# A transformer layer with 16 experts: each scatter of a sequence's sorted rows waits for the one before it

## The reference

```python
x = x + layernorm(attention(layernorm(x)))      # 16 heads, rotary positions, causal
x = x + layernorm(moe(layernorm(x)))

def moe(x):                                     # on n = 4096 tokens xf
    scores = sigmoid(xf @ gate_w.T)             # 16 experts in 4 groups
    # of the 4 groups the best 2 are kept, of their experts the best 4 (TOPK)
    topk_w = 2.5 * chosen / (chosen.sum() + 1e-20)
    hg, hu = xf @ Wg[e].T, xf @ Wu[e].T         # each expert: 256 -> 128
    y = sum over the 4 chosen e of topk_w * ((silu(hg) * hu) @ Wd[e].T)
    shared = (silu(xf @ Ws_g.T) * (xf @ Ws_u.T)) @ Ws_d.T
    return x + y + shared
```

## Time and profile before

| what | value |
|---|---|
| runs of the kernel, us | 983.48, 983.83, 987.33; median 983.83 |
| the profiled execution, span in us | 1048.8 |
| TensorE clock granted, mean | 0.888 of full speed |
| busy: PE / PEld / DVE / ACT / POOL, us | 852.6 / 615.2 / 652.3 / 456.3 / 426.7 |
| share of the span: PE / DVE / ACT / POOL | 81% / 62% / 44% / 41% |
| the scatters' DMA queue (q0): packets, MB | 13824, 38.55 |
| the other DMA queue (q1): packets, MB | 75248, 128.85 |

### The profile page before, as it was taken

How to read it: one execution, slowest core, us unless ns; L and a number is a source line. 1 busy time by engine, 2 the same in 40 slices (tenths; PEclk the granted TensorE clock), 3 DMA queues, 4 the chain that set the end, 5 groups by cost and what they waited for, 6 DMA issues and landing times.

```text
span 1048.8 us, 20609 instructions
## 1 busy us (share of the span) xinstructions
PE 852.6 (81%) x6580; PEld 615.2 (59%) x6580; DVE 652.3 (62%) x1914; ACT 456.3 (44%) x763; POOL 426.7 (41%) x408
## 2 busy tenths in 40 slices
PE   4569798987987987987987877978977799989955
PEld 3436374664664663664654545757865588867722
DVE  5577658687687687687586674533642233687916
ACT  2115454544544544544543555425433355544410
POOL 3222113135335335335213234374565555664621
PEclk9759898997897897997987998889999999998978
DMA  4685726236336336336395212453545566997783
GB/s 161 147 222 144 216 64 163 75 98 174 98 99 173 99 99 173 98 81 172 98 322 159 85 47 92 144 167 93 166 150 161 161 178 164 383 314 281 247 339 128
DMA packets 89175, 168.72 MB, mean 161 GB/s; under 512 B 14704, under 2 KB 56688, under 8 KB 88816
## 3 DMA queue, kind: packets, MB, share of 16 engines
q1 hardware_dynamic: 75248, 128.85, 42.1%
q0 software_dynamic: 13824, 38.55, 9.9%
HBM read 90.15 MB, written 76.68 MB: 159 GB/s over the span
## 4 chain that ended last, share of the span: by engine, by line
PE 40%; DVE 23%; issue 11%; SPq 8%; DMA 6%; another core or an unknown queue 5%; ACT 4%; POOL 3%; DVEq 0%; ACTq 0%; POOLq 0%
DVE nmax L829 8%; PE ring L1536 6%; PE ring L1314 5%; PE ring L1316 4%; PE ring L1315 4%; PE ring L1392 3%; PE ring L1557 3%; PE ring L1358 2%; SPq L628 2%; PE ring L1383 2%; SPq L629 2%; DMA xg<-sorted_rows 2%; PE ring L1436 2%; PE ring L1522 2%
## 5 line engine op out<-in xcount | busy, mean ns | idle before, releaser
L1244 ACT ACTIVATE prob<-ring 128x1024 f32<-128x1024 f32 (+1 forms) x192 | 167.5, 881 | 215.5 <-PE ring L1383 196.5
L829 DVE TENSOR_REDUCE nmax<-ring 128x2 f32<-128x1024 f32 (+3 forms) x256 | 201.8, 819 | 73.3 <-PE ring L1365 43.6
L736 POOL DMA_INDIRECT expert_rows<-ys,dest x160 | 159.2, 995 | 127.0 <-ACT ys L1198 74.8
L728 POOL DMA_INDIRECT sorted_rows<-xr,idx_all x128 | 130.5, 1019 | 104.8 <-DVE xr L991 71.5
L1536 PE MATMUL ring<-we,xh 128*128 x640 | 160.3, 396 | 0.0
L1536 PEld LDWEIGHTS ring<-we,xh 128*128 128x128 f32 x640 | 121.6, 200 | 14.6
L1054 DVE SCALAR_TENSOR_TENSOR sl<-sl,got,ring 128x128 f32<-128x128 f32 x160 | 48.3, 343 | 109.8 <-ACT sl L1296 62.5
L1358 PE MATMUL ring<-k_st,q_st 48*128 48x512 f32 (+3 forms) x512 | 88.9, 387 | 26.0 <-issue 9.7
L1392 PE MATMUL ring<-prob,v_sb 128*32 128x512 f32 (+3 forms) x1024 | 106.3, 518 | 3.2 <-ACT prob L1244 3.2
L1377 PE MATMUL ring<-maskt_b,halves_b 64*128 64x128 bf16 (+2 forms) x768 | 58.4, 233 | 50.7 <-DVE nmax L829 23.5
L1377 PEld LDWEIGHTS ring<-maskt_b,halves_b 64*128 64x128 bf16 x768 | 22.8, 97 | 125.4 <-issue 56.7
(11 more groups left out here) (203 smaller groups left out, 1650.8 us busy)
## 6 DMA issues: line engine op xcount, KB each, us to landing
xg<-sorted_rows SPq DMA_DIRECT2D x160, 134.0 KB
parts<-part SPq DMA_DIRECT2D x32, 512.0 KB
ykt<-expert_rows SPq DMA_DIRECT2D x14, 1024.0 KB
k_st<-parts SPq DMA_DIRECT2D x64, 128.0 KB
q_st<-parts SPq DMA_DIRECT2D x64, 128.0 KB
we<-w_exp SPq DMA_DIRECT2D x1, 6144.0 KB
sorted_rows<-zeros SPq DMA_DIRECT2D x2, 2144.0 KB, 9.6
sorted_rows<-zeros SPq DMA_DIRECT2D x32, 134.0 KB
```

The lines of the kernel that those rows point to most:

```text
L728: pool.indirect_dma_start(out=xs[group_of(s)], out_offset=bass.IndirectOffsetOnAxis(ap=idx_all[:, s, t, k:k + 1], axis=0), in_=xr[:, s % 2 ...
L736: pool.indirect_dma_start(out=yk, out_offset=bass.IndirectOffsetOnAxis(ap=dest[:, j % 8, b:b + 1], axis=0), in_=ys[:, j % NYS, b, :], in_o ...
L829: dve.tensor_reduce(nmax[:, Q % 2, :, pp, qb], slot[:, :, col:col + (qb + 1) * P], AX.X, ALU.max, negate=True).then_inc(s_max, 1)
L1244: act_e.activation(prob[:, u % 2, 2 * half:2 * half + 2, 0:width], slot[:, :, 0:width], ACT.Exp, scale=SCALE).then_inc(s_exp, 1)
```

## The change

Within a sequence, every scatter but the first waits until its predecessor has landed, that is until s_sc has the 16 of all scatters of this sequence before it. The number 256 * (s // 2) is what the earlier sequences of the same parity have added. The order of POOL's list, the destinations and the number of DMAs are the same. 15 of 16 scatters of each sequence, 120 in all, get the wait.

```diff
--- before.py
+++ after.py
@@ -725,6 +725,8 @@
                 if t == 0 and k == 0:
                     pool.wait_ge(s_place, PLACE_STEPS * (s + 1))
                     pool.wait_ge(s_xn2, NT * (s + 1))
+                else:
+                    pool.wait_ge(s_sc[s % 2], 256 * (s // 2) + 16 * (TOPK * t + k))
                 pool.indirect_dma_start(
                     out=xs[group_of(s)], out_offset=bass.IndirectOffsetOnAxis(ap=idx_all[:, s, t, k:k + 1], axis=0),
                     in_=xr[:, s % 2, t, :], in_offset=None).then_inc(s_sc[s % 2], 16)
```

## The result

The changed kernel takes 1040.26 us (median of 4 runs, 1037.16 to 1042.85) against 983.65 us for the kernel before (4 runs too): the ratio is 1.0576, with a 95% interval of 1.0553 to 1.0599. It is 56.6 us slower. The forecast was 10.7 us slower; the sign is right, the size is off by a factor of five, and the time lies outside the range.

What follows compares the result with a forecast made beforehand. The chain was read as 40% PE and 23% DVE, with POOL (3%) not the bound. Terms 2.8 + 2.4 + 1.0 + 2.5 + 1.5 + 0.5 = 10.7 us on 983.8 gave 994.5 us, range 981 to 1010 us.

Steps and rivals of the forecast that it cites:

- the base: Differences worked out on the 1048.8 us profiled execution, then added to the 983.83 us median of the runs.
- The burst of six: Scatters before a_lo in four attention windows: a_lo 3.6 us late, PE barely affected, 0.6 us each, 2.4 us together.
- The second layernorm's power: POOL step behind three scatters in four windows: 245.85 slips to about 248.4, DVE 2.0 us late; 2.8 us together.
- DVE's lateness reaches PE only in part: Same four windows: PE has other quads' matmuls queued, so nothing to half (1.0 us) reaches it, taken as 0.7 us.
- Sequences 4 and 5: Their scatters: sequence 4 mostly covered by idle time, 1.0 us; sequence 5 already on the chain, 2.5 us.
- Sequences 6 and 7: Scatters alternating with expert blocks' scatters: most waits find the predecessor landed; 1.5 us for sequence 6, 0.5 for 7.
- The sum's ends: All terms at their low end give about 3 us of cost, all at the high end about 22 us.
- The last four or five scatters: In the attention windows, the last four scatters have 20.28 us of POOL idle time behind them and cost nothing.
- The signs: Profile after: POOL gaps 1.2 to 1.6 us, 5 under full load; power 2 to 3 us later; a_lo directly behind its scatter.
- much slower: Rival: four burst landings at 6.3 us, second a_lo 5.4 us too late for PE in four windows; near 1014 us, chance 0.10.
- no effect: Rival: landings counted early, so waits are already met; 984 us, counted with the hidden case, together 0.22.
- faster: Rival: one scatter in flight thins out stalls without known releaser; half gone gives about 970 us, chance 0.12.

Runs made afterwards that it cites:

- e0: The kernel before, unchanged, run again for a second profiled execution: 986.22 us in one run, profiled span 984.4 us.
- e6: Against the kernel before, only scatters 5 to 10 of every sequence wait (48 of 120 waits): 1014.23 us, ratio 1.0304.
- e5: Against the kernel before, only scatters 1 to 4 of every sequence wait (32 of 120 waits): 1011.23 us, ratio 1.0265.
- e2: Against the kernel before, waits only in the scatters of sequences 4 and 5 (30 of 120): 998.89 us, ratio 1.0127.
- the first trace: The first profiled execution of the kernel before, which the prediction read: span 1048.8 us, with stalls without a known releaser.
- e3: Against the kernel before, waits only in the scatters of sequences 6 and 7 (30 of 120): 992.28 us, ratio 1.0088.
- e7: Against the kernel before, only scatters 11 to 15 of every sequence wait (40 of 120 waits): 985.08 us, ratio 1.0011.
- e4: Against the kernel before, each scatter waits for the one before its predecessor, so two may be in flight (112 waits): 984.20 us, ratio 0.9994.
- e8: All 120 waits, with POOL's list reordered for sequences 0 to 5 so its own steps precede the moved scatters: 1023.97 us, ratio 1.0412 to the kernel before.

## Why the prediction was wrong

**The step that failed first: the base.** The prediction worked "on the profiled execution" and added the difference to the median, though that trace was 65 us longer than the runs. It saw the stalls, asked whether they belong to the profiler, and allowed 1.3 us for it. But the stalls had opened room in the schedule that timed runs do not have: the first a_lo was 4.5 us later than in e0, PE's use of the second 5.3 us. POOL's waits were laid into that room. Of the 46 us that the sum lacks, the step from DVE to PE has some 14, the burst 14, most of them by the base, sequences 4 and 5 have 9, and sequences 6 and 7 have 7.

**The burst of six** was forecast to end at 270.4 with two landings under load and three without; it ended at 273.53 after a start 0.8 us later. The landings were 6.7, 4.5, 2.4, 2.5 and 4.7 us (the differences of the scatters' starts are 0.3 us more): the fifth met a second load. The mechanism was right and the price nearly so. With its own numbers the second a_lo ends at 274.3, and against e0's 271.40 that is 2.9 us too late in each window, 11.6 us (3.4 us a window when the two traces are laid on the scatter that opens the rows), where the sum had "0.6 us" a window. e6 measured 4.1 us a window.

**The second layernorm's power** was put 2.5 us late and DVE 2.0 us. The three landings ahead of it took 9.6 us and not 7.8, so the power was 3.6 us late in the first window, and DVE stood for it 2.98 to 4.35 us in the four windows of the changed kernel and 4.12 us in e5's first. What failed is "DVE's lateness reaches PE only in part", taken as 0.7 us. e5's windows are 4.3 us longer, as much as DVE was late: the row maxima that PE waits for stand behind these rows on DVE, and PE's other matmuls did not absorb it. Four windows: 17 us in place of 2.8 us.

**Sequences 4 and 5** were priced at 1.0 and 2.5 us; e2 measured 12 to 13. In e0 POOL has 7.47, 2.42 and 6.56 us of idle time before the two powers and the first a_lo in sequence 4's scatters, and 2.39, none and 2.51 us in sequence 5's; I set the room in sequence 4 against the idle price, 2.4 us. But the DMA engines are not idle there, as the first trace had it (windows as in the earlier trace rows; the last but one number is the share of the DMA engines):

```profile
540.00:548.00 8.00, 5.11 (x64) 3.27 (x60) 7.48 (x24) 2.14 (x3) 0.96 (x1) 0.77 0.88 208
548.00:553.00 5.00, 5.00 (x44) 2.75 (x45) 4.82 (x16) 2.82 (x4) 3.47 (x4) 0.50 0.96 199
```

The waits made a series of 11 landings, 8.4 us the longest, and the series ends after a_lo was due.

**Sequences 6 and 7** were 2.0 us and measured 9: two neighbours ahead of the last power were counted, but the power came 5.6 us later in e3. The four scatters that open the sequence are three more pairs; POOL's idle time behind them was 6.61 us in the first trace and 3.79 us in e0, and e3 uses it up. Behind that POOL works without a gap up to the power, so every neighbour there adds up. How the rest of the 9 us arises was not followed.

**The sum's ends** were added up a little wrong: the terms' low ends make 1.7 us and their high ends 23.6, where it has 3 and 22. Also, the load was read as high from 239 to 259 us without a break; from 242 to 248 the DMA engines were 0.14 busy. The measured 56.6 us lies outside either way.

**What held.** The last four or five scatters cost nothing (e7). The waits that stand behind two other DMAs of POOL mostly found the predecessor landed: in e3 17 of 30 were not waited for. The signs came: gaps of 1.63 to 2.14 us before the three scatters ahead of the lower parts, 5.84 us under load, DVE's idle time with POOL as its releaser in all four windows, and a_lo right behind its scatter; gaps of 3.76 and 4.01 us past 259 pointed to the much slower case. The landing is real and not counted early, so the "no effect" rival fell. Landings with little load took 2.4 to 2.5 us in these traces, loaded ones 4.5 to 8.4 us. The Trainium skill's fit ("DMA: Bandwidth & Descriptors", "Anatomy of one DMA — SWDGE (gpsimd) path") gives an estimate of 2.3 us for a scatter; the former agree with it, the latter do not, and by it alone the sum would have been 8 us. The "faster" rival fell with the stalls: e4, e7 and e0 have several scatters in flight and none of them. The "much slower" rival had the right mechanism, the second a_lo too late for PE in four windows, at 1014 us; it asked for four loaded landings and the full room of the first trace; three (6.7, 4.5 and 4.7 us) did it with the room of e0, and the other places came on top.

## What to carry to other kernels

Before a trace is used for a sum, hold its span against the timed runs: where it is several per cent longer, the room of every engine in it is wrong, not only its total, and a second trace is worth more than a correction. A wait in an in-order list is priced by the step that stands behind it and that step's room, not by the wait. If a DMA has to be held back, two in flight instead of one can make it free, as they did here (e4).

## What the hardware showed that was not expected

Landings under load overlap: the first two scatters of the burst had landed at most 9.0 us after the first one's start in e4; one after the other, they had landed 11.7 us after it in the changed kernel (250.43 to 262.15) and 12.2 us after it in e6 (247.70 to 259.85). The stretch decides the price, from 2.44 us to 8.38 us for 128 rows in the changed kernel, and to 10.74 us in e8, where the profile gives the DMA engines a share of 1.09 (510 to 521 us).

A stall may cost PE twice. Windows (us, busy us and instructions of PE, PEld, DVE, ACT and POOL, granted clock, DMA share, GB/s) of the changed kernel, where PE stood for a_lo, and then of e3 without waits there:

```profile
270.00:275.00 5.00, 2.03 (x30) 1.19 (x22) 3.83 (x11) 2.63 (x4) 2.23 (x2) 0.91 0.41 145
275.00:280.00 5.00, 2.27 (x11) 2.30 (x12) 1.39 (x5) 0.00 (x0) 4.41 (x4) 0.50 0.09 27
```

```profile
270.00:275.00 5.00, 5.00 (x34) 4.80 (x35) 4.33 (x14) 0.30 (x1) 2.88 (x3) 0.66 0.31 112
275.00:280.00 5.00, 5.00 (x56) 3.76 (x55) 4.01 (x10) 2.95 (x4) 0.00 (x0) 1.00 0.56 181
```

After PE had been busy for 2.03 of 5.00 us, the clock granted in the next stretch was 0.50, the lower of its two levels (1.2 GHz); in e3 it was 1.00 there. But e3 has a dip of its own in the stretch before, 0.66 with PE busy throughout, so this place alone does not show the price of a stall. Over the whole kernel PE was busy 834.1 us after and 825.2 us in e0 for the same 6580 matmuls, at a mean granted clock of 0.894 and 0.912: about 9 us of slower matmuls. How much of that is in the 56.6 us was not measured by itself.
